# S and T tiles in groups of three, three and two, and the products with V of two steps in one group

## The reference

```python
q = elu(q) + 1.0; k = elu(k) + 1.0          # 16 heads, D = 16
q = _apply_rope(q, sin, cos); k = _apply_rope(k, sin, cos)
attn = softmax(einsum('bhnd,bhmd->bhnm', q, k) * D ** -0.5)
attn_out = einsum('bhnm,bhmd->bhnd', attn, v)
x = _layernorm(x + attn_out + lepe(v))       # lepe: 3-tap depthwise conv
h = concatenate([x, -x]); h = relu(s0 * (h @ sign(k0))) * 2
h = relu(s1 * (h @ sign(k1))) * 2
x = _layernorm(x + s2 * (h @ sign(k2)))
```

## Time and profile before

| | |
|---|---|
| median of 3 runs | 2095.31 us (2095.06 to 2096.69) |
| profiled execution, its own time | 2094.53 us |
| its span, first to last instruction | 2092.4 us |
| TensorE busy | 2043.8 us (98%) |
| VectorE busy | 1685.7 us (81%) |
| ScalarE busy | 1489.0 us (71%) |
| GpSimd busy | 1013.3 us (48%) |
| mean granted TensorE clock | 0.985 |

### The profile page before, as it was taken

One profiled execution on the slowest core, in us unless ns is written; L12 is line 12 of the kernel. 1 busy time (PEld: TensorE's weight loads), 2 busy tenths in 40 slices (PEclk: granted clock), 3 DMA queues, 4 the chain that ended last, 5 costly groups with the idle time before them and its releaser, 6 DMA issues.

```text
span 2092.4 us, 43715 instructions
## 1 busy us (share of the span) xinstructions
PE 2043.8 (98%) x17150; PEld 802.9 (38%) x17150; DVE 1685.7 (81%) x3094; ACT 1489.0 (71%) x2867; POOL 1013.3 (48%) x583
## 2 busy tenths in 40 slices
PE   5999999999999999999999999999999999999998
PEld 3132323343433434334343343434343343434355
DVE  8989988788887988888887888878888788888143
ACT  3399888766877678776787767777687766867642
POOL 2968287614757158462585328661475704300010
PEclk7699999999999999999999999999999999999999
DMA  5001210020010200021000200002001010000000
GB/s 199 20 17 47 72 24 31 22 72 13 15 37 31 80 16 16 30 77 42 9 27 27 89 22 17 29 16 99 12 17 37 29 62 17 17 9 29 1 21 21
DMA packets 40429, 76.87 MB, mean 37 GB/s; under 512 B 15024, under 2 KB 19488, under 8 KB 37280
## 3 DMA queue, kind: packets, MB, share of 16 engines
q1 hardware_dynamic: 34496, 49.97, 8.3%
q0 software_dynamic: 5184, 23.07, 3.0%
q10 hardware_dynamic: 544, 1.05, 0.1%
HBM read 46.27 MB, written 25.17 MB: 34 GB/s over the span
## 4 chain that ended last, share of the span: by engine, by line
PE 86%; DVE 8%; ACT 3%; issue 1%; SPq 0%; DMA 0%; POOL 0%; POOLq 0%; ACTq 0%
PE unit_banks L761 27%; PE unit_banks L625 22%; PE o_bank L670 22%; PE unit_banks L697 5%; PE unit_banks L774 5%; DVE maxima L1032 5%; ACT probs L855 2%; PE unit_banks L685 2%; PE unit_banks L635 2%; DVE hT L1101 1%; PE unit_banks L678 1%; ACT rows L943 0%; DMA lepe_rows<-in_b_v 0%; ACT work L897 0%; DVE rows L1161 0%
## 5 line engine op out<-in xcount | busy, mean ns | idle before, releaser
L1032 DVE TENSOR_REDUCE maxima<-unit_banks 128x1 f32<-128x512 f32 x2048 | 1302.5, 682 | 285.4 <-PE unit_banks L625 281.7
L855 ACT ACTIVATE probs<-unit_banks 128x512 f32<-128x512 f32 x2048 | 1115.5, 605 | 491.1 <-PE unit_banks L635 487.6
L625 PE MATMUL unit_banks<-k_stack,q_stack 48*128 48x512 f16 x2048 | 636.5, 388 | 6.2 <-DVE maxima L1032 2.7
L635 PE MATMUL unit_banks<-q_stack,k_stack 50*128 50x512 f16 x2048 | 634.0, 383 | 5.3 <-ACT probs L855 3.2
L670 PE MATMUL o_bank<-probs,v_pair 128*32 128x256 f32 x8192 | 565.3, 387 | 4.0 <-issue 4.0
L761 PE MATMUL unit_banks<-h0T,w 128*128 128x512 f16 x2048 | 480.2, 380 | 0.1
L1439 POOL TENSOR_TENSOR attn<-o_rows_sb,rden 128x256 f32<-128x256 f32 x63 | 39.2, 622 | 743.1 <-DVE rden L1045 739.5
L670 PEld LDWEIGHTS o_bank<-probs,v_pair 128*32 128x32 f32 x8192 | 207.0, 109 | 306.3 <-issue 206.0
L625 PEld LDWEIGHTS unit_banks<-k_stack,q_stack 48*128 48x128 f16 x2048 | 121.8, 94 | 433.2 <-issue 241.3
L761 PEld LDWEIGHTS unit_banks<-h0T,w 128*128 128x128 f16 x2048 | 188.6, 98 | 249.3 <-issue 55.6
L1104 DVE SCALAR_TENSOR_TENSOR h1T<-unit_banks,h1T 128x512 f16<-128x512 f32 x128 | 87.3, 682 | 77.9 <-ACT h1T L919 77.8
(11 more groups left out here) (151 smaller groups left out, 1677.8 us busy)
## 6 DMA issues: line engine op xcount, KB each, us to landing
rows<-in_x POOLq DMA_DIRECT2D x8, 1024.0 KB, 6.3
q_stack<-q_scratch SPq DMA_DIRECT2D x128, 64.0 KB, 2.0
k_stack<-k_scratch SPq DMA_DIRECT2D x128, 64.0 KB, 2.0
work<-in_xT SPq DMA_DIRECT2D x7, 1024.0 KB, 8.1
q_scratch<-parts POOLq DMA_DIRECT2D x14, 512.0 KB, 3.3
k_scratch<-parts POOLq DMA_DIRECT2D x14, 512.0 KB, 3.2
out<-rows SPq DMA_DIRECT2D x7, 1024.0 KB, 4.9
q_stack<-q_scratch SPq DMA_DIRECT2D x128, 32.0 KB, 1.9
```

The lines of the kernel that those rows point to most:

```text
L625: nc.tensor.matmul(units.out(unit), q_stack[row:row + STACK, r, t * P:(t + 1) * P], k_stack[row:row + STACK, r, half * 512:(half + 1) * 51 ...
L635: nc.tensor.matmul(units.out(unit), k_stack[row:end, r, kt * P:(kt + 1) * P], q_stack[row:end, r, half * 512:(half + 1) * 512], start=True ...
L855: nc.scalar.activation(probs[:, 2 * (kt % 2) + h, half * 512:(half + 1) * 512], units.out(unit), ACT.Exp, scale=exp_regs[2 * (n % PAIRS) + ...
L1032: nc.vector.reduce_max(maxima[:, v // T % 2, h * T + t, half:half + 1], units.out(unit), AXIS_X)\
```

## The change

- TensorE: the four pairs of tiles of a step are taken by column halves (head 0 and 1 of half 0, then of half 1: tile i has S of head i % 2 and T of head 1 - i % 2, half i // 2). Own units, dense pieces and early products stand before tile 0 in even steps and before tile 1 in odd ones; the products of two steps stand together behind tile 1 of even steps. So the groups of tiles have two, three and three pairs in two steps. Where a step has no dense work, one half step of products stands in that place.
- `probs` becomes a ring of five half steps (`HALVES`) for both heads; it was two whole steps.
- ScalarE and VectorE follow tile by tile, with their side work (`side_work`) behind tile 1 of even and tile 0 of odd steps, and the readings of dense units behind tile 0 of even and tile 1 of odd ones on VectorE (before that tile on ScalarE).
- The V ring has three pairs, not four, `o_rows_sb` one buffer, not two. The planner follows the new order.

```diff
+V_RING = 3
+HALVES = 5
-COPY_V_AT = {3: (0, 1, 2, 3, 4, 7), 1: (7,), 5: (7,)}
+COPY_V_AT = {3: (0, 1, 2, 3, 4, 5), 1: (7,), 5: (7,)}
+def done_in(s):
+    return [u for u, part in DEALT[s] if ends_unit((u, part))]
+def early_products(s):
+    if DEALT[s] or s == 0:
+        return []
+    if s % 2 == 1:
+        return [2 * s - 2] if (s - 1) % T != 0 else []
+    return [2 * s - 4 + len(early_products(s - 1))]
+def products_behind(s):
+    return range(2 * s - 4 + len(early_products(s - 1)) + len(early_products(s)), 2 * s) if s > 0 else ()
...
-WRITING = {"S": 0.25, "T": 0.25, "PV": 0.9, ...
+WRITING = {"S": 0.25, "T": 0.25, "PV": 0.45, ...
...
-        v_pair = sb("v_pair", [P, RING, T, 2, 32], F32)
+        v_pair = sb("v_pair", [P, V_RING, T, 2, 32], F32)
-        probs = sb("probs", [P, 4, N], F32)
+        probs = sb("probs", [P, 2 * HALVES, N // 2], F32)
-        o_rows_sb = sb("o_rows_sb", [P, 2, 512], F32)
+        o_rows_sb = sb("o_rows_sb", [P, 512], F32)
...
+            def score_tiles(s, i):
+                if s + T + LEAD < STEPS:
+                    scores(s + T + LEAD, i % 2, i // 2)
+                scores_T(s, 1 - i % 2, i // 2)
...
-                scores_both(s, 0)
-                for unit in own_units(s):
-                    if unit[0] == "O rows":
-                        o_rows(unit)
-                    else:
-                        max_rows_T(unit)
-                for unit, part in DEALT[s]:
-                    dense(unit, part)
-                if s > 0 and not DEALT[s]:
-                    weighted_v(s - 1, 0)
-                    if kt == 0:
-                        weighted_v(s - 1, 1)
-                scores_both(s, 1)
-                if s > 0 and DEALT[s]:
-                    weighted_v(s - 1, 0)
-                    weighted_v(s - 1, 1)
-                elif s > 0 and kt > 0:
-                    weighted_v(s - 1, 1)
-            for half in range(2):
-                weighted_v(STEPS - 1, half)
+                for i in range(4):
+                    if i == (1 if s % 2 == 1 else 0):
+                        for unit in own_units(s):
+                            if unit[0] == "O rows":
+                                o_rows(unit)
+                            else:
+                                max_rows_T(unit)
+                        for unit, part in DEALT[s]:
+                            dense(unit, part)
+                        for x in early_products(s):
+                            weighted_v(x)
+                    score_tiles(s, i)
+                    if i == 1 and s % 2 == 0:
+                        for x in products_behind(s):
+                            weighted_v(x)
+            for x in range(2 * STEPS - 4 + len(early_products(STEPS - 1)), 2 * STEPS):
+                weighted_v(x)
...
-                    wait(act, pv_done, 2 * (s - 2) + half + 1)
+                    wait(act, pv_done, x - HALVES + 1)
...
-                wait(act, attn_written, n - 1)
-                nc.scalar.activation(o_rows_sb[:, n % 2], units.out(unit), ACT.Copy).then_inc(units.free_sem(unit), 1)
+                wait(act, attn_written, n)
+                nc.scalar.activation(o_rows_sb[:], units.out(unit), ACT.Copy).then_inc(units.free_sem(unit), 1)
...
-                wait(act, pv_done, 2 * (n - RING + 1) * T)
+                wait(act, pv_done, 2 * (n - V_RING + 1) * T)
...
+                for tile in range(4):
+                    if tile == s % 2:
+                        if kt == O_ROWS_STEP and n > 0:
+                            copy_o_rows(n - 1)
+                        for unit in done_in(s):
+                            if unit[0] == "proj":
+                                elu_inputs(unit)
+                            elif unit[0] in HIDDEN:
+                                high_part(unit)
+                    exp_probs(s, tile)
+                    if tile == 1 - s % 2:
+                        side_work(s)
...
+                for tile in range(4):
+                    if v < STEPS:
+                        row_max(v, tile % 2, tile // 2)
+                    if tile == 0:
+                        for unit in own_units(s):
+                            if unit[0] == "max rows":
+                                split_max_rows(unit[1])
+                    if tile == s % 2:
+                        for unit in done_in(s):
+                            dense(unit)
+                    if tile == 1 - s % 2:
+                        side_work(s)
```

## The result

| | before | after |
|---|---|---|
| median | 2095.18 us (2093.55 to 2096.69, 4 runs) | 2163.85 us (2161.39 to 2164.82, 4 runs) |
| profiled execution, its own time | 2094.53 us | 2163.67 us |
| its span | 2092.4 us | 2161.5 us |
| mean granted TensorE clock | 0.985 | 0.986 |

The kernel became slower: ratio 1.0326, 95% interval 1.0308 to 1.0344, 69 us. The forecast was 2158. The clock is the same, so the difference is work or waiting.

A forecast was written before the change was run, and what follows sets the result against it. TensorE's stream was taken to set the pace. From the profiled 2094.5 us, fewer groups took 50, T tiles alone 5, and bank waits added 118: 2157.5, as a median 2158 us, range 2112 to 2194.

The forecast's parts named there:

- What bounds: In steady state TensorE's stream is the kernel's clock; only what shortens or interrupts it counts.
- Fewer groups: Tiles and products: fewer changes of kind save 0.24 per two steps at 209 places, 50 us.
- T alone: Last twelve steps, without S: neighbouring T tiles use both row halves, 0.9 x 6 = 5 us gained.
- Alternating row halves: Inside groups, S takes the half the T tile before had; pairs stay 0.22 apart, no cost.
- Banks: Behind or inside groups of three, TensorE waits for a bank still being read: 118 us lost at 247 places.
- The 0.41: Time lost per wait for the first S tile's bank: next matmul 1.16 after the group's start, not 0.75.
- the 0.1 at 40 places: Behind 40 of the 45 groups meeting two held banks, the next unit waits about 0.1 more: 4 us.
- Pairs without dense work: 41 two-step units lacking dense work on one or both sides: saving counted 0, bounds -10 and +10 us.
- Buffers: Five half steps of exponentials, V ring of three, one o_rows buffer: no waits, all 0.
- The sum: Whole kernel: 2094.5 - 50 - 5 + 118 = 2157.5, median 2158 us.
- The saving comes through: Rival: first tile's bank isn't awaited or is read within 0.75 of the group's start; 2040 us, chance 0.09.
- VectorE falls behind: Rival: VectorE's work with two L0 units per step adds 0.2 per wait, 49 us; 2207 us, chance 0.08.

The follow-up runs named there:

- e3: Changed kernel, with the row maximum of the first S tile of each group of three reading 256 of its 512 columns: 2096.11 us (ratio 1.0003 to the kernel before).
- e4: Changed kernel, with the row maximum of the second S tile of each group of three reading 256 of its 512 columns: 2154.5 us (ratio 1.028).
- e10: Kernel before, with only the last twelve steps' T tiles in alternating heads, so that two run in both row halves: 2090.16 us (ratio 0.9971).
- e2: Changed kernel, with waits for loaded stacks, loaded and joined maxima and copied O taken one tile earlier: 2154.07 us (ratio 1.0277 to the kernel before).
- e9: The order of e7, with products split around a pair of tiles at 96 even steps: 2081.6 us (ratio 0.9933 to the kernel before).
- e6: Kernel before, with six banks for the planner in place of seven: 2132.47 us (ratio 1.0179).
- e1: Changed kernel, with even steps' own units, dense pieces and early products put ahead of the previous odd step's last tile: 2125.27 us (ratio 1.0142).
- e7: The order of e1, with max rows a step later and finished units read before the tile that follows them: 2125.0 us (ratio 1.0145).

## Why the prediction was right, point by point

*What bounds.* Right: only what interrupts TensorE's stream counted. The idle sixth of VectorE's time did not help, because the wait is the latency of one read (e3, e4).

*Fewer groups.* Right to a hundredth: a group of three takes 0.76 (forecast 0.75), four half steps of products 1.87 (1.86), and a steady batch's products fell by 4.5 us, 32 x 0.14. The tiles without their waits fell from 68.7 to 65.9, 2.8 where 32 x 0.10 = 3.2 was counted. (Before, 2.6 us of a batch's 71.3 were already lost, at steps 14, 15 and 20 to 22.)

*T alone.* Right: two T-only steps with two dense pieces went from 7.81 to 6.92, 0.89, where 0.9 was counted; in e10, which has the alternating heads alone, they take 6.96.

*Alternating row halves.* Right: pairs in swapped halves stand 0.22 apart in after, too (658.19, 658.41, 658.63). By the rule in the Trainium skill ("TensorE: Matmul & The Clock Gate", Part 3, The mechanism) that a weight load overlaps a running matmul only in another row group, they would stand further apart; the measurement decides.

*Banks.* Right in mechanism; the price of a place was too small, and waits of the kernel before, which had been left out, made up for it. By the kernel's own plan of banks, 216 groups of three have something behind them that takes the bank of the group's first S tile (152 + 50 = 202 were counted), and 45 a sixth tile that takes a bank of its own group (45 counted). In the trace 190 of the 216 and all 45 last over 0.1 longer than 0.76, and with them 14 whose successor takes the bank of the group's first T tile: 249 places, where 247 were counted. They cost 92 + 38 + 6 = 136 us, where 118 was counted. The 0.41 holds at 33 of the 190, where the wait for the bank is alone; at 157 it was 0.5, at most of them for the second semaphore (e2 brought some 135 down); and seven of the 45 lost 1.4 and not 0.72. Behind two held banks nothing more was lost: the 0.1 at 40 places was zero. In a steady batch 20.8 us were lost at 38 places, where 118 / 247 a place makes 18.1. Against that stand 2.6 us that before lost in each steady batch and that are gone, so 18.2 net. The prediction did not see them: it took the ten waits of the line for L625 in the earlier trace rows for all waits for maxima (the full list has five more, of T tiles, and one of rows of O; with them it is 4.2 us), and a lost time shows there only in part. That the term came out right is in this part luck. The Trainium skill ("TensorEngine Tiling (Array Packing)", PSUM Bottleneck) says that tiling speeds up TensorE but not the emptying of PSUM. The trace agrees: the pairs come at 0.22, a bank's read stays at 0.68.

*Pairs without dense work.* Counted at 0, bounds 10 either way. Batches 0 and 1 grew by 3.1 and 9.3, together 3.3 more than my terms give; e4 shows that in batch 0 VectorE's load plays a part. How much of the 3.3 is this, and how much the same bank waits, wasn't separated.

*Buffers.* Right: products waited for exponentials 0.2 us in the whole span, and neither the V ring nor the single `o_rows_sb` appears among TensorE's waits.

*The sum.* Steady batches grew by 11.0 each (10.4 forecast), batch 7 with what follows it by 0.9 (1.4), and 0.7 lies ahead of the first T tile. The 2158 was 6 short: about 3 from the five steady batches and 3 from the first two. Both traces have one stretch at the lower clock in batch 1, so the clock has no part in the 69.

*The rivals.* "The saving comes through" fell at the wait of 0.41 that it denied. It is what e9 shows once most waits are out of the way, though not at 2040: its 96 splits cost some 0.3 each, and batches 0 and 1 still hold most of the waits that are left. Of "VectorE falls behind" the runs show batch 0, where less work for VectorE is worth 6 to 7 us whichever read it is taken from (e4, e3), and about 1 in batch 7.

## What to carry to other kernels

Where a group of instructions takes n banks and what stands behind it needs one more, count n + held units + 1 against the banks that there are, in each place of the order: beyond that, the price is the latency of one read (here 0.41, or 0.50 with a second semaphore), even with a reader that is idle for a fifth of the time. The count gave 8 of 7 banks for the new order and 6 of 7 for the old one. It isn't the whole of it: with six banks the old order has 6 of 6 at its usual steps and still lost 37 us (e6), part of it at steps with an extra unit. The price can be more than what longer groups save (here 0.24 per two steps). Moving the successor alone took away 39 us and moved other waits to the group's own last tile (e1, e7); putting work that needs no bank between the tiles removes those, for 0.32 a place (e9).

When two kernels differ by some microseconds, the granted clock of each stretch should be compared first: four stretches of 3.4 us at the lower clock hid what e7 had saved.

## What the runs showed of the hardware beyond this

- A second semaphore cost TensorE time although it was fulfilled 16 us before: 0.15 us from the end of the read to the matmul, where 0.06 is usual. Taking it one tile earlier gave 10 us in the whole kernel.
- One bank fewer cost 179 us with groups of three and 37 with groups of two.
- Two T tiles of different heads take 0.32 up to the products that follow, two of one head 0.54.
- A stretch of 3.4 us at the lower level of the granted clock made a steady batch 1.6 us longer (e6, 253.3 and 254.9). Which runs have how many was not the same from kernel to kernel; what sets it was not tested.
